# Block outputs of the second half of the attention by Strassen's scheme: seven products for eight

## The reference

```python
x = x + attention(layernorm(x))
# attention, with wuk = w_uk.reshape(H, 128, 128), wuv = w_uv.reshape(H, 128, 128), H = 32:
c_q = h @ w_q_down                          # 384 wide
c_kv = h @ w_kv_down                        # 128 wide, keys and values of all heads
scores = (q_nope @ wuk) . c_kv + rope(q_rope) . rope(k_rope)
probs = softmax(where(causal, scores / sqrt(192), lowest))
out_lat = einsum('bhst,btr->bhsr', probs, c_kv)
out = einsum('bhsr,hdr->bhsd', out_lat, wuv)
return out.reshape(b, s, H * 128) @ w_out   # 1024 wide
```

## Time and profile before

| | us |
|---|---|
| median of 3 runs | 2042.65 |
| lowest and highest | 2042.39, 2043.1 |
| span of the profiled execution | 2041.3 |
| PE busy in it | 2036.0 |
| DVE busy | 1190.8 |
| ACT busy | 778.8 |
| POOL busy | 491.0 |

### The profile page before, as it was taken

How to read it: one execution, slowest core, us unless ns; L and a number is a source line. 1 busy time by engine, 2 the same in 40 slices (tenths; PEclk the granted TensorE clock), 3 DMA queues, 4 the chain that set the end, 5 groups by cost and what they waited for, 6 DMA issues and landing times.

```text
span 2041.3 us, 29819 instructions
## 1 busy us (share of the span) xinstructions
PE 2036.0 (100%) x10640; PEld 1722.9 (84%) x10640; DVE 1190.8 (58%) x1977; ACT 778.8 (38%) x2031; POOL 491.0 (24%) x453
## 2 busy tenths in 40 slices
PE   9999999999999999999999999999999999999999
PEld 7788888888888888888888888888888778888887
DVE  6766666666666666665666666666567772332322
ACT  5443535344444444333333333333333455232221
POOL 5442424233333333211221222122221311000000
PEclk9999999999999999999999999999999999999999
DMA  9846445353535353585424435242344481202011
GB/s 361 331 138 225 141 146 182 104 190 100 185 107 179 107 199 114 209 300 176 150 66 149 133 99 174 72 154 81 130 139 186 146 308 42 83 0 83 1 42 42
DMA packets 69219, 294.52 MB, mean 144 GB/s; under 512 B 7329, under 2 KB 8097, under 8 KB 59553
## 3 DMA queue, kind: packets, MB, share of 16 engines
q1 hardware_dynamic: 69152, 293.64, 42.1%
HBM read 182.99 MB, written 110.62 MB: 144 GB/s over the span
## 4 chain that ended last, share of the span: by engine, by line
PE 99%; DVE 0%; DMA 0%; ACT 0%; issue 0%; DVEq 0%; ACTq 0%; SPq 0%
PE at_out L53 12%; PE at_out L55 12%; PE at_out L54 11%; PE at_qbank L55 7%; PE at_qbank L53 7%; PE at_qbank L54 7%; PE at_qbank L1168 6%; PE at_qbank L1169 6%; PE at_score L944 6%; PE at_score L942 3%; PE at_turned L950 3%; PE at_value L55 2%; PE at_value L54 2%; PE at_value L53 2%; PE at_value L1185 1%; PE at_value L1186 1%
## 5 line engine op out<-in xcount | busy, mean ns | idle before, releaser
L1912 DVE TENSOR_TENSOR at_acc<-at_out,at_acc 128x512 f32<-128x512 f32 x512 | 352.2, 688 | 116.3 <-PE at_out L55 109.9
L53 PE MATMUL at_out<-at_wvo,at_val_hi 128*128 128x512 f32 x1024 | 414.1, 404 | 0.0
L55 PE MATMUL at_out<-at_wvo,at_val_lo 128*128 128x512 f32 x1024 | 401.4, 392 | 0.0
L54 PE MATMUL at_out<-at_wvo,at_val_hi 128*128 128x512 f32 x1024 | 400.1, 391 | 0.0
L1325 ACT ACTIVATE at_probs<-at_probs,at_row_stats 128x128 f32<-128x128 f32 x512 | 199.8, 391 | 353.7 <-DVE at_row_stats L1890 353.7
L1603 POOL TENSOR_TENSOR at_probs<-at_probs,at_row_stats 128x512 f32<-128x512 f32 x128 | 133.1, 1040 | 586.0 <-DVE at_row_stats L1895 586.0
L55 PEld LDWEIGHTS at_out<-at_wvo,at_val_lo 128*128 128x128 f32 x1024 | 192.2, 188 | 44.3
L54 PEld LDWEIGHTS at_out<-at_wvo,at_val_hi 128*128 128x128 f32 x1024 | 193.3, 189 | 33.8
L53 PEld LDWEIGHTS at_out<-at_wvo,at_val_hi 128*128 128x128 f32 x1024 | 193.1, 189 | 33.9 <-DVE at_acc L1912 0.5
L1331 ACT ACTIVATE at_pT_hi<-at_turned 128x512 fp32r<-128x512 f32 x128 | 76.3, 596 | 317.1 <-PE at_turned L950 317.1
L1903 DVE TENSOR_TENSOR at_val_lo<-at_value,at_val_hi 128x512 fp32r<-128x512 f32 x128 | 88.5, 691 | 179.1 <-ACT at_val_hi L1335 179.1
(11 more groups left out here) (236 smaller groups left out, 4134.7 us busy)
## 6 DMA issues: line engine op xcount, KB each, us to landing
wvo_d<-at_wvo SPq DMA_DIRECT2D x16, 2048.0 KB, 10.4
parts_d<-at_rope_parts SPq DMA_DIRECT2D x32, 1024.0 KB, 7.1
at_qrope<-parts_d SPq DMA_DIRECT2D x128, 256.0 KB, 5.4
at_wvo<-wvo_d SPq DMA_DIRECT2D x16, 2048.0 KB, 8.4
ab_raw<-in_w_heads SPq DMA_DIRECT2D x32, 576.0 KB, 6.1
cr_ctx<-in_context SPq DMA_DIRECT2D x32, 512.0 KB, 6.6
wabs_d<-at_wabs SPq DMA_DIRECT2D x16, 768.0 KB, 8.0
at_wabs<-wabs_d SPq DMA_DIRECT2D x16, 768.0 KB, 5.4
```

Source lines behind the costliest of these rows:

```text
L53: pe.matmul(out, w_hi, x_hi, start=first, stop=False)
L54: pe.matmul(out, w_hi, x_lo, start=False, stop=False)
L55: return pe.matmul(out, w_lo, x_hi, start=False, stop=last)
L1912: dve.tensor_tensor(at, outb[n][:], at, ALU.add).then_inc(added, 1)
```

## The change

In the second group (m = 8 to 15) the outputs of a step are seen as a 2 x 2 product: two batches by two heads of values, times two heads by two column halves of weights. It is made by a Strassen scheme with seven block products, each in three passes: 21 matmuls of 512 columns for 24. `slot` is split: `slot_first` for group 0 keeps the eight products, `slot_second` has the seven.

The seven products go to the two banks so that a bank is read several times while sums run on in it:

```diff
+    FACTORS = {"P1": (A11, "b11", 0), "P2": (A12, "b21", 1), "P6": (S2, "t2", 0), "P5": (S1, "t1", 0),
+               "P7": (S3, "t3", 1), "P3": (S4, "b22", 0), "P4": (A22, "t4", 1)}
...
+            def product(m, s, name, start=False):
...
+                pe.matmul(out, hi, weight[:, 0], start=start, stop=False, skip_group_check=True)
+                pe.matmul(out, hi, weight[:, 1], start=False, stop=False, skip_group_check=True)
+                if name == "P1":
+                    pe.wait_ge(val_lo_done, STEPS * m + s + 1)
+                pe.matmul(out, lo, weight[:, 0], start=False, stop=True, skip_group_check=True).then_inc(out_ready, 1)
...
+            def slot_second(m, s, end, kind, first):
+                next_scores(m, s, end, kind, first)
+                product_1(m, s)
+                if s + 1 < end:
+                    turn(m, s + 1)
+                product_2(m, s)
+                product_6(m, s)
+                next_latent(m, s, end, kind, first)
...
+                    product_5(m, s)
+                    product_7(m, s)
+                if s + 1 < end:
+                    values(m, s + 1, group_of(kind, s + 1))
...
+                product_3(m, s)
+                product_4(m, s)
+                if s in ROPE_AT and end > STEPS:
+                    next_rope(m, s, kind, first)
```

The sums of the values are made on DVE from a whole copy of the bank (`val_whole`, in SBUF), all four of these instructions with both inputs in SBUF; ACT and POOL cut the sums. In the next piece `value_sums` is DVE's, `direct_values` ACT's and `slot_second` POOL's:

```diff
+            def value_sums(m, s):
+                done, of = 3 * later(m, s), val_whole[s % 2]
+                dve.wait_ge(val_in, later(m, s) + 1)
+                dve.tensor_tensor(of[:, S1], of[:, A22], of[:, A21], ALU.add).then_inc(val_sums, 1)
...
+                dve.tensor_tensor(of[:, S2], of[:, S1], of[:, A11], ALU.subtract).then_inc(val_sums, 1)
...
+            def direct_values(m, s):
+                act.wait_ge(value_ready, STEPS * m + s + 1)
+                act.activation(val_whole[s % 2][:, 0:CH], value[:], ACT.Copy).then_inc(val_in, 1)
+                act.wait_ge(val_in, later(m, s) + 1)
+                act.activation(val_hi[s % 2][:, DIRECT], val_whole[s % 2][:, DIRECT], ACT.Copy).then_inc(val_hi_done, 1)
...
+            def slot_second(m, s, end, kind, first):
+                finish = s - 1 in ROPE_AT and end > STEPS
+                add(m, s, 0)
+                if finish:
+                    rope_sums(first + USE[kind][s - 1] + 3)
+                add(m, s, 1)
+                if finish:
+                    rope_low(m + 1, ROPE_AT[s - 1])
+                if s + 2 < end:
+                    normalise(m, s + 2)
+                if s + 1 < end:
+                    value_sums(m, s + 1)
```

More of the change, by code:

```diff
@@ L1064, in slot @@
                 output(m, s, 1)
-                if s in ROPE_AT and end > STEPS:
-                    if kind == "full":
-                        pe.wait_ge(wqr_lo, m + 2)
-                    else:
-                        pe.wait_ge(wqr_in, 16 * (m - QUADS + 2))
-                        if kind == "switch":
-                            pe.wait_ge(cq_in[ROPE_AT[s]], 16)
-                    rope(ROPE_AT[s], use[s] + 1, first + use[s])
+                if s in ROPE_AT:
+                    next_rope(m, s, kind, first)
                 if part:
@@ L1220, in _ @@
             opening()
[L1221 removed]
+            quads(pe, slot_first, slot_second, beside_last)
             cross()
@@ L1422, in slot @@
                     cut_half(0, i, count)
-                if s + 2 < end:
-                    exps(m, s + 2)
-                if s // 2 + 2 < end // 2:
-                    latent(m, s // 2 + 2, s % 2, use[s])
-                if s + 1 < end:
+                if of := making(kind, s):
+                    make_high(m + of[0], of[1])
+                exps(m, s + 2)
+                latent(m, s // 2 + 2, s % 2, use[s])
+                if part and what == "B":
+                    cut_half(1, i, count)
+                if kind == "switch" and s + 1 == STEPS:
+                    direct_values(m + 1, 0)
+                    value_sums(m + 1, 0)
+                else:
                     values(m, s + 1)
@@ L1430, in slot @@
                     rope_keys(N - 1)
-                if part and what == "B":
-                    cut_half(1, i, count)
-                if s - 1 in ROPE_AT and end > STEPS:
-                    c = ROPE_AT[s - 1]
-                    rope(m + 1, c, 16 * (m + 1 + c))
+                if s - 1 in ROPE_AT:
+                    rope(m + 1, ROPE_AT[s - 1])
                 if part:
@@ L1450, in slot @@
                     act.activation(wqr[:, 0], wqr_raw, ACT.Copy).then_inc(wqr_hi, 1)
+            def slot_second(m, s, end, kind, first):
+                keep(m, s, "P1")
+                if s + 1 < end:
+                    turn(m, s + 1)
+                keep(m, s, "P2")
+                if s + 2 < end:
+                    exps(m, s + 2)
+                if s // 2 + 2 < end // 2:
+                    latent(m, s // 2 + 2, s % 2, USE[kind][s])
+                if s - 1 in ROPE_AT and end > STEPS:
+                    rope(m + 1, ROPE_AT[s - 1])
+                if s + 1 < end:
+                    direct_values(m, s + 1)
+                    value_sums(m, s + 1)
             def cross_normalise(b):
@@ L1644, in opening, with slot_first @@
                 rope_low(0, 1)
-            def slot(m, s, end, kind, first):
-                finish = s - 1 in ROPE_AT and end > STEPS
+                make_low(0, 0, LOWS[:1])
+            def slot_first(m, s, end, kind, first):
+                finish = s - 1 in ROPE_AT
                 part = absorbed(kind, s)
@@ L1658, in slot @@
                     cut_half(m, s, 1, (AHEAD + part[3]) % 2)
-                if s + 2 < end and not opens(m, s):
+                if not opens(m, s):
                     normalise(m, s + 2)
@@ L1983, in opening, with slot_first @@
                 dve.sem_inc(added, 2)
[L1984 removed]
+                take_head(0, 2, first + 8, 8)
                 keys(N - 1)
[L1987 removed]
+            def slot_first(m, s, end, kind, first):
                 use = USE[kind]
[L1989 to L1994 removed]
+                turn(m, s + 1)
+                largest(m, s + 2)
+                add(m, s, 0, 0)
                 if opens(m, s):
```

506 lines of the change are left out of this document (359 added, 147 removed).

## The result

| | before | after |
|---|---|---|
| median, us | 2042.52 | 2060.07 |
| lowest and highest | 2042.22, 2043.1 | 2059.48, 2061.48 |
| span of the profiled execution | 2041.3 | 2057.7 |

The ratio is 1.0087, with a 95% interval of 1.0073 to 1.0101, from four runs of each. The page of the changed kernel, to set beside the earlier trace rows: busy time, and the chain that ended last, by engine.

The account below looks back on a forecast made before the run. PE was taken as the bound, busy 2036.0 of 2041.3 us. Span 2041.3 - 1.4 (seven quads) + 5 (last quad) + 1 (first group) + 1 (switch) = 2046.9, with 1.35 outside 2048.2, called 2048; own range 2030 to 2062, with rivals 2015 to 2062.

Parts of the forecast that it names:

- rival (b): First group: DVE's adds come 0.8 later than walked, two steps in each of eight quads stall; 13 more, 2061; chance 13%.
- What goes: Second group: three matmuls of 0.229 us fewer in each of 64 steps; 5.5 us a quad, 44 in all.
- the 0.4 a quad for gaps: Second group: loss from a second change from short transposes to a long product within a step, at half of 0.09.
- DVE and POOL exclude each other: Second group: four DVE instructions reading SBUF twice each wait for the end of what POOL has begun.
- The plain step: Second group, no rope in it or the step ahead: PE stalls 0.25 us before P1 (0 to 0.6), four times a quad.
- The step behind a rope step: Second group, steps 2 and 5: sums wait for POOL, PE stalls 1.95 us before P1 (1.3 to 2.8), twice a quad.
- The last quad: Quad without rope: late adds and sums stall PE for 10 us, less the 5.5 won; 5 lost (2 to 9).
- First group and switch: First group: added DVE work makes adds late, 1 us (0 to 6); switch: first sums and weights, 1 us (0 to 3).
- loads: nothing: Loads issued two steps, 19 us, before need cost nothing; up to 3 a quad if the relayout holds SP.
- (a): Second group: sums and POOL do not meet, seven quads win 31, last loses 3, rest costs 2; 2017; chance 22%.
- (c): Half and half: plain steps do not stall and the last quad loses 2; 2038 or a little less; chance 12%.
- (d): Whole kernel: PE idles enough for its clock to fall to 1.2 GHz; some 2100; chance 3%.

Follow-up runs that it names:

- the runs without the exclusion: Changed kernel with the three value sums and the direct values' low part reading one input from PSUM instead of SBUF: 2021.08 us, ratio 0.9894.

## Why the prediction was right, and where not

The forecast was 2048, its own range 2030 to 2062, and slower by over 0.2% was its likelier sign (0.46). The time fell into both ranges and on that side, 12 us over the forecast and 2 below the upper end of the ranges. The mechanism was right; that the time stayed in the range has some luck in it, since about half of the 12 us come from the first quad, where none was forecast. The 2061 of rival (b) lies nearest of all to the measured time, and that is chance: its cause did not occur.

**What goes: right.** 5.5 us a quad. With all cover restored that is what a quad wins. The gap between transposes and a product was taken at half of 0.09 for P2. It is a whole one (P2 takes 0.78 from 1268.16 to 1268.94, P6 then 0.70), but it costs nothing: the scores, which now stand behind a product and no longer behind the transposes, take 1.27 (1091.82 to 1093.09 above) and not the 1.36 that the walk kept from the earlier trace rows. The two cancel, and the step without a stall is 9.39, the 9.38 of the matmuls alone. So the 0.4 a quad for gaps should have been none.

**DVE and POOL exclude each other: right**, and the reason that the kernel got slower. The sizes of the undisturbed sums were estimated at 0.29, 0.42 and 0.56; they are 0.29, 0.42 and 0.55, and the shorter sums that the prediction set beside this, with 0.3 us less for them together, did not come. Open was whether the normalisation, with an input repeated along the columns, holds DVE too. It does (0.88 for 0.29 above). The Trainium skill, in "SBUF — State Buffer", section "SBUF: two separate sides", counts every GpSimd instruction that reads SBUF, and the trace agrees with it at each of the three sums. It also says that the holding goes both ways: whichever instruction starts first keeps the other out. The fourth instruction shows that side. The cut of the direct values is never held (0.54 to 0.56 in all 64), and POOL's low part (1.48 from 1276.99) begins while DVE still cuts them and is 0.19 longer than the 1.29 it has when these read PSUM. The walk of the plain step had this, as a later start of POOL's; that of the step behind rope left it out.

**The plain step: mechanism right, size too small.** 0.25 was forecast before P1, 0.49 measured. Part of it is the 0.09 above: PE wants P1 earlier than the walk had it. The rest is the step that failed, the walk from P7 to the reciprocal. It had POOL's normalisation begin at 8.60 behind the scores; it began at 9.04 (1274.28, the scores of that step being at 1275.14 less 9.90), since the stall itself, the whole gap at P2 and the adds of P5 and P7 one behind the other (1.42 us) all push it. The second of them needs the sum of the first, since both go to the same part of `acc`. As I read it, the loop from P1 over `values` and the sums to the next P1 is what sets the step, and each part of it that is 0.1 longer adds 0.1; no run lengthened one part alone. Bounds of 0 to 0.6 held it.

**The step behind a rope step: right.** The walk gave a stall of 1.9 and I took 1.95; P1 starts 3.19 behind the scores there (1219.21 to 1222.40), which is 1.9 over 1.28, with the three waits that were walked. The quad came to 89.2 for a forecast of 88.5 and 88.75 before. The forecast had 9.68 for each of four plain steps (9.38, 0.05 of gap, 0.25 of stall) and they take 9.90: 0.9 more. The gap charged to the other four steps is 0.2 too much. Over seven quads that is +3.2 instead of -1.4.

**The last quad: right**, 5.7 for 5; PE waits there up to 1.5 us for P6's add:

```profile
1591.25 0.50 PE L1086 MATMUL at_out<-at_wvo,at_val_hi 128*128 128x512 f32 x1 [1.51 <-DVE at_acc L2221]
```

**First group and switch:** for the quads in the loop 0.1 each, within the 1 us. The switch cost nothing, for 1. But the first quad cost 6.4, with a forecast of none. The step that failed is "loads: nothing": I held the new stores and loads against the steady order, and did not walk the one quad that is written apart. There the store of t4 is issued at 153.90, 4.4 us before DVE wants its buffer back, and `rope_tmp` has got a second user, which delays a load by 6 us; that was in the diff as a change of name only. These two waits are 2.8 us of the 6.4; what the other 3.6 are stays open.

**The rivals.** (a), *the cover holds*, had no chance as the change was written, but it was priced well: it gave 84.3 a quad and the runs without the exclusion show 84.2. (b) would have been visible as 0.5 and more in each quad of the first group; there is 0.1. (c) is out: the plain steps do stall, and the last quad lost 5.7 and not 2. Of (d) there is a trace of 4 us only, in the first quad.

The 12 us are thus 4.6 in the seven quads, 4.9 in the first group with the switch (6.9 for 2), 0.7 in the last quad, 0.5 behind it, and 1.0 outside the span (2060.07 less 2057.7 is 2.4, where 1.35 was taken as fixed; the profiled execution was the shortest of the four, 2059.48).

## What to carry to other kernels

A VectorE instruction with both inputs in SBUF, however short, cost here what was left of the GpSimd instruction beside it. If one of its inputs still stands in PSUM, read it there, and put GpSimd's work of no hurry behind that which VectorE meets. Where a saving on the bounding engine does not show, look at what the replacing work waits for before giving the saving up: here the change lost 18 us as it was made and wins 30 of the 44 us of matmuls with the same products. One changed operand brought 39 us and one changed order on POOL 6 more. In seven quads the matmuls are won in full; the last quad, the first one and what lies behind keep the rest. Walk the first and the last round of a loop by themselves, and for each buffer that changes its place ask who used the new place before and which load that delays.

## What the runs showed of the hardware that was not expected

- Short idle times and the clock: after 3.3 us of idle PE in the first quad the granted clock fell to 0.50 for some 3 to 4 us. In the kernel with only the early store PE waited at three places there, for 1.1, 1.7 and 1.8 us, and the clock stayed at 1.00 in all its windows from 160 to 184 us. Both took 2060 us. It is not a rule that split waits leave the clock alone: with the same early store and the sums from PSUM, PE waited there for 1.3 and 1.7 us and then for 0.6, and the clock fell all the same, to 0.50 from 167 to 168 us, with matmuls of 0.63 us for 0.39.
- For VectorE a 128-column sum takes 0.29 us with an input in PSUM and 0.28 to 0.29 with both in SBUF and POOL idle: the place of the input makes no difference at this size.
